# A scan-based recurrence on one core: the fp32 product of gate and tanh moves from VectorE to GpSimd, and VectorE adds each step's output

## The reference

```python
def step(carry, xs):
    h, c = carry
    xi_t, xf_t, xg_t, xo_t = xs
    i_t = jax.nn.sigmoid(xi_t + h @ V_i)
    g_t = jnp.tanh(xg_t + h @ V_c)
    o_t = jax.nn.sigmoid(xo_t + h @ V_o)
    c_new = h * c + i_t * g_t
    h_new = o_t * jnp.tanh(c_new)
    return ((h_new, c_new), h_new)
...
t = t + _L2_ffn_ref(_ln_t(t), ...)
```

## Time and profile before

| | |
|---|---|
| median of 3 runs (lowest to highest) | 1300.95 us (1299.09 to 1301.1) |
| the profiled execution | 1295.79 us |
| its span, first to last instruction | 1294.0 us |
| mean granted TensorE clock | 0.783 |
| busy: PE, DVE, ACT, POOL | 990.2, 843.1, 514.9, 279.6 us |

### The profile page before, as it was taken

How to read it: one execution, slowest core, us unless ns; L and a number is a source line. 1 busy time by engine, 2 the same in 40 slices (tenths; PEclk the granted TensorE clock), 3 DMA queues, 4 the chain that set the end, 5 groups by cost and what they waited for, 6 DMA issues and landing times. The chain is left out here.

```text
span 1294.0 us, 23970 instructions
## 1 busy us (share of the span) xinstructions
PE 990.2 (77%) x8107; PEld 545.6 (42%) x8107; DVE 843.1 (65%) x2435; ACT 514.9 (40%) x1332; POOL 279.6 (22%) x393
## 2 busy tenths in 40 slices
PE   6878777677999666666666666658964999999996
PEld 2466552253667344444444444433522333333332
DVE  7787647735566645555555555554366888888885
ACT  3544534353444333333333333334532454545542
POOL 4604102200000100000000000000000465555655
PEclk9889988878999955555555555558986999999998
DMA  7000002000000000000000000000004655646550
GB/s 238 1 2 1 1 2 82 0 1 1 3 1 1 1 2 0 0 0 0 0 0 0 0 0 0 0 0 3 0 1 98 147 126 119 137 113 134 123 123 9
DMA packets 11251, 47.52 MB, mean 37 GB/s; under 512 B 1840, under 2 KB 6320, under 8 KB 6704
## 3 DMA queue, kind: packets, MB, share of 16 engines
q1 hardware_dynamic: 11184, 46.62, 14.9%
HBM read 43.99 MB, written 2.62 MB: 36 GB/s over the span
## 5 line engine op out<-in xcount | busy, mean ns | idle before, releaser
L2169 ACT ACTIVATE ex_gated<-wide,unscale 128x1024 f32<-128x1024 f32 x128 | 142.2, 1114 | 139.4 <-PE wide L2135 139.3
L2185 DVE TENSOR_TENSOR ex_hid<-wide,ex_gated 128x1024 f32<-128x1024 f32 x128 | 155.8, 1222 | 39.2 <-ACT ex_gated L2169 27.9
L1694 PE MATMUL wide<-h,vh 128*128 128x16 f16 x768 | 63.3, 181 | 152.2 <-DVE h L1759 152.2
L2111 POOL TENSOR_TENSOR ex_acc<-ex_part,ex_acc 128x512 f32<-128x512 f32 x120 | 152.6, 1272 | 95.3 <-DVE ex_part L2201 81.3
L1749 DVE TENSOR_TENSOR_SCAN cells<-terms 128x48 f32<-128x48 f32 x256 | 75.3, 294 | 111.2 <-ACT terms L1715 108.9
L1715 ACT ACTIVATE terms<-wide 128x32 f32<-128x32 f32 x256 | 54.6, 213 | 211.0 <-PE wide L1698 211.0
L1694 PEld LDWEIGHTS wide<-h,vh 128*128 128x128 f16 x768 | 40.3, 108 | 221.1 <-DVE h L1759 221.1
L2147 PE MATMUL wide<-ex_hid,w 128*64 128x512 f32 x512 | 116.7, 598 | 0.0
L2135 PE MATMUL wide<-xh,wh 64*128 64x512 f16 x512 | 99.0, 383 | 5.1 <-PEq L83 3.7
L1730 POOL TENSOR_TENSOR ls_hx<-ls_hs,h_unscale 128x128 f32<-128x128 f32 x32 | 14.6, 455 | 395.3 <-DVE ls_hs L1760 395.3
L2135 PE MATMUL wide<-xh,wl 64*128 64x512 f16 x512 | 98.3, 380 | 0.0
(11 more groups left out here) (368 smaller groups left out, 1941.4 us busy)
## 6 DMA issues: line engine op xcount, KB each, us to landing
ex_d<-route SPq DMA_DIRECT2D x64, 512.0 KB, 6.5
par_attn<-in_attn SPq DMA_DIRECT2D x1, 2704.0 KB, 13.3
par_rest<-in_rest SPq DMA_DIRECT2D x1, 2523.5 KB, 18.7
L_xin<-in_x SPq DMA_DIRECT2D x8, 256.0 KB, 5.8
w<-in_w SPq DMA_DIRECT2D x1, 2048.0 KB, 8.2
out<-ex_acc SPq DMA_DIRECT2D x16, 128.0 KB, 3.3
w<-in_w SPq DMA_DIRECT2D x1, 512.0 KB, 9.1
route<-ro_dt SPq DMA_DIRECT2D x2, 256.0 KB, 2.0
```

Of the source, the lines that this page charges most:

```text
L1694: pe.matmul(ig[:, g, :] if g < 2 else o, v[:, g, :], h1[:], start=False, stop=False, skip_group_check=True)
L2111: pool.tensor_tensor(acc[:, t % 2, :], part[:, (e // 2) % 2, e % 2, :], acc[:, t % 2, :] if e else tile_of(m.xa, t), ALU.add)\
L2169: act.activation(gated[:, n % 2, :], pair_of_up(n // GS, 2 * (n % GS))[:], ACT.Silu, scale=m.unscale[:, 0:1]).then_inc(s["gated_ready"], 1)
L2185: dve.tensor_tensor(hid[:, n % (2 * GS), :], pair_of_up(n // GS, 2 * (n % GS) + 1)[:], gated[:, n % 2, :], ALU.mult).then_inc(s["hid_ready ...
```

## The change

Three things are done in the recurrence. Pool no longer scales and adds whole chunks; `hs`, `hx` and `h_unscale` go. Instead DVE adds each step's output to `xa` itself, as h32 / SC + xa, behind hc. And h32 is formed by Pool, in one buffer `h32`, while DVE forms h1; Pool waits for tc, then for og and for DVE's addition of the step before. In front of h2 DVE waits for h32 and for its own h1. Where there are several waits, the one for the event that comes last is written first.

```diff
-                pool.memset(m.h_unscale[:], 1.0 / HSCALE).then_inc(s["cleared"], 1)
...
-        hs = sb("hs", [P, 2 * STEPS, HB])
-        hx = sb("hx", [P, 2, STEPS, HB])
+        h32 = sb("h32", [P, HB])
...
         @block.gpsimd
         def _(pool):
-            pool.sem_inc(s["scaled"], 2)
             with pool.Fori(0, HW // (2 * STEPS)) as i:
                 for b in range(2):
-                    j = 2 * i + b
-                    pool.wait_ge(s["h32_ready"], STEPS * (j + 1))
-                    pool.tensor_tensor(hx[:, b], hs[:, STEPS * b:STEPS * (b + 1), :], unscale[:], ALU.mult)\
-                        .then_inc(s["scaled"], 1)
-                    pool.wait_ge(s["scaled"], j + 3)
-                    x = xa_bt[:, :, bass.ds(STEPS * j, STEPS)]
-                    pool.tensor_tensor(x, hx[:, b].rearrange("p s b -> p b s"), x, ALU.add).then_inc(s["out_ready"], 1)
+                    for q in range(STEPS):
+                        t = 2 * STEPS * i + STEPS * b + q
+                        pool.wait_ge(s["tc_ready"], t + 1)
+                        pool.wait_ge(s["og_ready"], t + 1)
+                        pool.wait_ge(s["out_ready"], t + 1)
+                        pool.tensor_tensor(h32[:], og[:], tc[:], ALU.mult).then_inc(s["h32_ready"], 1)
 
         @block.vector
...
+            dve.sem_inc(s["out_ready"], 1)
...
-                    dve.wait_ge(s["scaled"], 2 * i + b + 1)
...
                         dve.wait_ge(s["tc_ready"], t + 1)
                         dve.wait_ge(s["og_ready"], t + 1)
-                        h32 = hs[:, STEPS * b + q, :]
                         dve.tensor_tensor(h1[:], og[:], tc[:], ALU.mult).then_inc(s["h1_ready"], 1)
-                        dve.tensor_tensor(h32, og[:], tc[:], ALU.mult).then_inc(s["h32_ready"], 1)
                         dve.wait_ge(s["h32_ready"], t + 1)
-                        dve.tensor_tensor(h2[:], h32, h1[:], ALU.subtract).then_inc(s["h2_ready"], 1)
-                        dve.scalar_tensor_tensor(hc, h32, 1.0 / SC, cell, ALU.mult, ALU.mult)\
+                        dve.wait_ge(s["h1_ready"], t + 2)
+                        dve.tensor_tensor(h2[:], h32[:], h1[:], ALU.subtract).then_inc(s["h2_ready"], 1)
+                        dve.scalar_tensor_tensor(hc, h32[:], 1.0 / SC, cell, ALU.mult, ALU.mult)\
                            .then_inc(s["hc_ready"], 1)
+                        x = xa_bt[:, :, bass.ds(t, 1)].rearrange("p b t -> p (b t)")
+                        dve.scalar_tensor_tensor(x, h32[:], 1.0 / SC, x, ALU.mult, ALU.add)\
+                           .then_inc(s["out_ready"], 1)
                         if b == 1 and q == 3:
```

More of the change, by code:

```diff
@@ L1649, in lstm_stage @@
         names = ("warm z_done zo_done o_ready gates_ready cell_ready tc_ready og_ready h1_ready h32_ready h2_ready "
-                 "hc_ready scaled out_ready").split()
+                 "hc_ready out_ready").split()
         u, bias, vh, vl, h1, h2 = m.u, m.ls_bias, m.vh, m.vl, m.h1, m.h2
-        terms, cells, unscale, factors, addends = m.terms, m.cells, m.h_unscale, m.factors, m.addends
+        terms, cells, factors, addends = m.terms, m.cells, m.factors, m.addends
         sem = c.enter_context(StageSemaphores(nc, "ls"))
@@ L2280, in build @@
                                     ("vl", [3, P], F16), ("ls_bias", [P], F32), ("terms", [2, HB * 3 + 2], F32),
-                                    ("cells", [HB, 3], F32), ("h_unscale", [8, HB], F32), ("h1", [HB], F16),
+                                    ("cells", [HB, 3], F32), ("h1", [HB], F16),
                                     ("h2", [HB], F16)):
@@ L2284, in build @@
             m.u, m.vs, m.vh, m.vl, m.ls_bias = (setup[n] for n in "u vs vh vl ls_bias".split())
-            m.terms, m.cells, m.h_unscale, m.h1, m.h2 = (setup[n] for n in "terms cells h_unscale h1 h2".split())
+            m.terms, m.cells, m.h1, m.h2 = (setup[n] for n in "terms cells h1 h2".split())
             flat = m.terms[:].rearrange("p z n -> p (z n)")
```

## The result

The changed kernel takes 1313.57 us (median of 4 runs, 1312.89 to 1314.57) beside 1300.02 us for the kernel before (4 runs, 1298.93 to 1301.1): a ratio of 1.0105, 95% interval 1.0087 to 1.0122. That is 13.55 us slower.

A forecast was written before the change was run, and what follows sets the result against it. Each step was taken as one closed chain across engines, not limited by any engine's throughput. Later h2 starts, +23.0 us, less 10.0 for Pool's chunk work, put +13.0 on 1300.95: 1314 us, range 1305 to 1326.

The forecast's parts named there:

- Pool's chunk work: Chunk ends: removing Pool's two instructions ends stretched scans, -9.3 us, and shortens the stage's end, -0.7; together -10.0 us.
- x on DVE: Each step, behind hc: DVE's addition to xa costs nothing, with 0.24 us of cover before the scan.
- Pool's product: h32 on Pool: starts 0.08 us behind the tanh, takes 0.22 us, ready at 0.30 us as before; neutral.
- The wait on h32: In front of h2: a register instruction carries the wait, so h2 starts 0.12 us after Pool's end instead of 0.04.
- The sum: Whole recurrence: h2 0.09 us later per step, +23.0 us, with -10.0 gives +13.0 us.
- A: Rival at the wait before h2: h2 itself carries the wait on h32, giving 1293.5 us; chance 0.12.
- B: Rival at Pool's h32: Pool is held until h1 ends, +0.23 us per step, 1350 us; chance 0.06.
- C: Rival at Pool's h32: product much cheaper, 0.17 us, whole level at 1301 us; chance 0.05 with small mixes of A.

The follow-up runs named there:

- e2: Kernel before with only DVE adding each step's output; h32 stays on DVE, Pool has no work in the stage: 1289.02 us, ratio 0.9924.
- e1: Changed kernel with the count t + 2 formed earlier, at the wait on o_ready in front of og: 1288.75 us, ratio 0.9918.
- e3: Kernel before with one line added, the wait on h1_ready behind the wait on h32_ready in front of h2: 1324.37 us, ratio 1.0197.
- e5: e1 plus a 128x512 two-input DVE product behind og in one step of 16, under way when Pool's product starts: 1293.04 us, one execution.
- e4: Changed kernel with the two waits in front of h2 swapped, h1_ready first and h32_ready second: 1305.35 us, ratio 1.0044.

## Why the prediction was right, point by point

The forecast was 1314 us; 1313.57 was measured.

*Pool's chunk work.* Predicted -9.3 us for the scans and -0.7 at the end. The scans no longer stretch, and e2, which does this and the addition on DVE without the rest, shows 9.0 us between the first and the last h1. At the end, DVE's last addition starts at 888.0 and takes 0.18 us, 0.8 us behind the last h1 (887.4), where Pool's ended 1.5 behind the earlier trace rows. The next stage follows it: its first instruction (ACT L1213) starts 1.5 us behind the last h1, where it was 2.3. Confirmed.

*x on DVE.* Predicted at nothing, with 0.24 us of cover. It ends 0.37 us ahead of the scan in the step shown, 0.13 better than reckoned, as it started just 0.19 us behind h2. In e2 and in the changed kernel no scan is longer than 259 ns. The 16 steps with the reduction behind `xa` take 1.674 us (median), like the rest, so taking nothing for them was right too. Confirmed.

*Pool's product.* Predicted 0.08 us behind the tanh and 0.22 long; measured 0.08 and 222 ns. The row of 8 columns in the earlier trace rows was the right neighbour, and the fixed part of a Pool instruction carries nearly all of it. e1 against e2 prices the move at 0.004 us a step. Confirmed: neutral. The forecast had said itself that no row of 16 columns was there; its bounds, 0.19 to 0.26, were 18 us wide in the total.

*The wait on h32.* Predicted: a register instruction carries it, and h2 starts 0.12 us behind Pool's end. The trace shows just that, e3 shows it without Pool, e1 takes it away. The source for it was a pair of rows from another stage, the same copy with a counted and with a constant wait.

*The sum.* 0.09 us a step were predicted. The step grew from 1.578 to 1.675, 0.097 us. The difference of 0.007 us a step, 1.7 us in all, is within what times read at 10 ns leave open, and some 0.4 us of it are the return of the loop, below. So the recurrence and its end grew by 14.7 us (15.4 less 0.7), where 13.0 were predicted. That the medians differ by 13.55 us, and that the forecast was met within 0.5 us, is in part luck: with 14.7 us in the recurrence the other stages must have come out 1.2 us shorter, and they vary by more than that.

*The rivals.* A, the faster one, fails in the change as it is written, but its mechanism is what e1 produces: h2 carries the wait and starts 0.04 us behind Pool's end. Its time, 1293.5, was 4.8 us above the 1288.75 measured. B, Pool held by h1, does not occur as a full hold: Pool takes 0.22 us, not 0.36. Whether a hold of some 10 ns hides in the 222 ns can't be told, as no run has this product without h1 beside it. But the reason that the prediction gave against it was too wide: from an unhurt hx behind h2 it read that Pool is not held by an earlier DVE instruction. e5 shows that it is held by a long one. That Pool is not held here because h1 is short fits both, and it fits hx, which is no longer behind h2 (0.455 us) than ahead of it (0.453 in e3); no run varied the length of h1. C falls with the 222 ns.

## What to carry to other kernels

Look not only at which wait is written first, but at which instruction carries it. In this loop a wait for a count that was not in a register yet put a register instruction behind the wait in front of it, and the late event then cost 0.09 us more. Form the count earlier, at a wait that has slack. Price the halves of a change apart, too: moving the output to DVE was worth 10 us, moving h32 to Pool nothing, and a wait that came with the second half cost 23. And when an edit moves an instruction by 0.1 us, look again at what it now runs beside, as h2 and hx in e3.

## What the runs showed of the hardware that was not expected

A wait for an event long past cost 25 us in e3, nearly all of it through the register instruction that it brought along. This was expected in kind; the runs give the three prices side by side, from the event to the start of h2: 0.12 us with the register instruction in between (e3 and the changed kernel), 0.10 with a semaphore instruction (e4), and 0.03 to 0.04 where h2 carries the wait itself (e1 and the kernel before).

A shift of 0.08 us made h2 2.5 times as long: it took 0.17 us when it started 0.04 us ahead of Pool's 128-column product, and 0.44 us when it started 0.04 us behind it (e3). Pool's product took 0.455 and 0.453 us.

A two-input DVE instruction of 512 columns held a Pool product of 16 columns for 0.18 us (0.406 against 0.222), and the product ended just 0.08 us behind the DVE instruction (e5).

At the return of the loop, once in 16 steps, the changed kernel loses a little. In this timeline of DVE, the first of 15 returns, the next h1 comes 1.72 us after the last, not 1.675; in the other 14 it is 1.69 to 1.70 us:

```profile
485.45 0.17 DVE L1754 TENSOR_TENSOR h<-ls_og,ls_tc 128x16 f16<-128x16 f32 x1 [0.22 <-ACT ls_tc L1719]
...
486.62 0.26 DVE L1745 TENSOR_TENSOR_SCAN cells<-terms 128x48 f32<-128x48 f32 x1 [0.42 <-ACT terms L1713]
...
487.17 0.17 DVE L1754 TENSOR_TENSOR h<-ls_og,ls_tc 128x16 f16<-128x16 f32 x1 [0.22 <-ACT ls_tc L1719]
```

Here the scan starts 0.78 us behind h2, elsewhere 0.74 (0.76 in the other 14). Over 15 returns this is some 0.4 us; its cause was not tried.
